# A fused expert, attention and FFN kernel: first FFN product in full rows and 32-row tiles, fp32 rows for q, k and v, v and projection in strips

## The reference

```python
x = x + conv(_gn(x))            # per token: 5 experts of 96x96, the top 2 mixed, leaky relu
t = tokens(x)                   # 16 images x 256 tokens x 96
t = t + attn(_ln_t(t))          # 6 heads of 16, causal
t = t + ffn(_ln_t(t))
...
k = jnp.einsum('btc,hcd->bhtd', x, wk)     # and q, v with wq, wv
out = out.transpose(0, 2, 1, 3).reshape(B, T, C) @ wproj + bproj
...
h = jax.nn.gelu(jnp.einsum('bsd,edh->ebsh', x, w1) + b1[:, None, None, :], approximate=False)
y = jnp.einsum('ebsh,ehd->ebsd', h, w2) + b2[:, None, None, :]
out = jnp.einsum('bse,ebsd->bsd', masked, y)      # masked: softmax gates of the top 2 of 4 experts
```

## Time and profile before

| what | value |
|---|---|
| median of 3 runs | 325.53 us (324.63 to 330.4) |
| profiled execution, its own time | 328.99 us |
| its span | 327.2 us |
| PE busy | 305.1 us, 93% |
| VectorE busy | 242.6 us, 74% |
| ScalarE busy | 217.8 us, 67% |

### The profile page before, as it was taken

The page is one execution under the profiler, slowest core; times in us unless marked ns, Lnnn a source line. Parts: engine busy times, 40 slices in busy tenths (PEclk is TensorE's granted clock), DMA queues, the critical chain, the costliest instruction groups (busy, mean ns, idle before and its releaser), DMA issues.

```text
span 327.2 us, 9038 instructions
## 1 busy us (share of the span) xinstructions
PE 305.1 (93%) x3300; PEld 240.6 (74%) x3300; DVE 242.6 (74%) x1058; ACT 217.8 (67%) x443; POOL 106.9 (33%) x179
## 2 busy tenths in 40 slices
PE   4889888799799999999998999899999999999995
PEld 2655535567679878888876877778887888888884
DVE  5868889888799889998998787368678743653423
ACT  3879676769596895887656844836489398176730
POOL 4563565558600471083070144410442014010000
PEclk9999999989999999999999999989999999999999
DMA  7900072504301120024052006400140010000000
GB/s 181 191 17 1 24 121 62 87 0 107 44 2 40 51 61 2 4 75 99 1 111 63 2 3 125 49 2 1 51 100 3 24 29 2 2 27 2 2 26 24
DMA packets 24199, 14.88 MB, mean 45 GB/s; under 512 B 14399, under 2 KB 24155, under 8 KB 24156
## 3 DMA queue, kind: packets, MB, share of 16 engines
q1 hardware_dynamic: 24156, 14.32, 20.8%
HBM read 3.11 MB, written 1.57 MB: 14 GB/s over the span
## 4 chain that ended last, share of the span: by engine, by line
PE 55%; DVE 9%; SPq 8%; DMA 5%; issue 3%; POOL 2%; ACT 2%; DVEq 0%; POOLq 0%; ACTq 0%
PE PS L974 17%; SPq L497 8%; PE PS L776 7%; PE PS L777 6%; PE PS L778 6%; DMA k_stack<-qk_parts 5%; PE PS L878 3%; PE PS L920 3%; PE PS L902 2%; PE PS L967 2%; PE PS L867 2%; PE PS L829 2%; PE PS L932 1%; PE PS L934 1%; PE PS L906 1%
## 5 line engine op out<-in xcount | busy, mean ns | idle before, releaser
L974 PE MATMUL PS<-w_f,hidden 128*64 128x96 f32 x1536 | 72.1, 251 | 0.0
L769 ACT ACTIVATE hidden<-PS 128x512 f32<-128x512 f32 x96 | 53.5, 599 | 27.2 <-PE PS L778 25.8
L974 PEld LDWEIGHTS PS<-w_f,hidden 128*64 128x64 f32 x1536 | 65.9, 139 | 6.4 <-issue 6.4
L1226 DVE SCALAR_TENSOR_TENSOR res<-PS,weight,res 128x96 f32<-128x96 f32 x128 | 31.4, 309 | 30.4 <-PE PS L974 30.2
L776 PE MATMUL PS<-t_hi,w_hi 97*128 97x512 f32 x96 | 41.7, 435 | 0.0
L1134 DVE CUSTOM_DVE_ANT_0 masked<-PS,causal 128x128 bf16<-128x128 f32 (+1 forms) x120 | 34.9, 352 | 4.3 <-PE PS L878 3.5
L777 PE MATMUL PS<-t_lo,w_hi 96*128 96x512 f32 x96 | 38.1, 397 | 0.0
L778 PE MATMUL PS<-t_hi,w_lo 97*128 97x512 f32 x96 | 38.0, 396 | 0.0
L746 ACT ACTIVATE prob_a<-PS 128x512 f32<-128x512 f32 x48 | 26.0, 600 | 13.4 <-PE PS L902 13.2
L631 POOL TENSOR_SCALAR_AFFINE_SELECT prob_a<-prob_a 128x768 f32<-128x768 f32 x16 | 13.8, 864 | 62.0 <-ACT prob_a L746 62.0
L1095 DVE SCALAR_TENSOR_TENSOR PS<-conv_y,weight,PS 128x96 f32<-128x96 f32 x128 | 30.3, 315 | 1.8 <-ACT PS L698 1.6
(11 more groups left out here) (169 smaller groups left out, 698.7 us busy)
## 6 DMA issues: line engine op xcount, KB each, us to landing
q_stack<-qk_parts SPq DMA_DIRECT2D x48, 96.0 KB, 3.2
k_stack<-qk_parts SPq DMA_DIRECT2D x48, 96.0 KB, 3.7
out_dram<-res SPq DMA_DIRECT2D x8, 192.0 KB, 2.3
X<-in_x_dram SPq DMA_DIRECT2D x4, 192.0 KB, 3.1
X<-in_x_dram SPq DMA_DIRECT2D x2, 384.0 KB, 5.6
hidden<-in_L_ffn_w_dram SPq DMA_DIRECT2D x1, 576.0 KB
w_f<-in_L_ffn_w_dram SPq DMA_DIRECT2D x1, 576.0 KB
hidden<-in_L_conv_We_dram SPq DMA_DIRECT2D x1, 180.0 KB
```

What stands on the lines that cost most here:

```text
L769: act.activation(hidden[:, m, 0:T * P], PS[:, bank("ffn1", n, index), 0:T * P], ACT.Gelu).then_inc(act_emptied["ffn1"], 1)
L974: mm = pe.matmul(PS[strip:strip + STRIP, y, t * C:(t + 1) * C], hidden[:, m, t * P + strip:t * P + strip + STRIP], w2_f[:, m, :], start=Fa ...
L1226: ins = dve.scalar_tensor_tensor(res2[:, t, :], PS[:, y, t * C:(t + 1) * C], weight1[:, t, e:e + 1], res2[:, t, :], ALU.mult, ALU.add).the ...
```

## The change

Five edits, and a new order for all engines:

- `ffn1`: the 3 x 96 rows of the three products are packed. One full matmul of 128 rows holds the 96 high-by-high rows and 32 rows of the low weights, the second the 96 low-by-high rows and another 32, and the last 32 rows of high by low go to a separate matmul with a 32-row operand. The new step `rest1.e` issues these for the three blocks of expert e in a row, from partitions 0, 32 and 64 and into three banks, which stay open until then. b1 becomes the bias of the Gelu.
- The packed rows are laid out by DMA. `t2@n` on SP issues five for each unit once ACT has copied `norm2_t` out, and the first `ffn1` block of the unit waits for all five; `w_w1` issues six for the weights, once.
- `qk` is one fp32 matmul of 512 columns for each of q and k. `v` is fp32 too, in strips of 64 rows; so is `proj`. No low part is made for the first norm, and DVE's `norm1_t` step and GpSimd's `w_qkv` are gone.
- The gate bias is added by DVE in an operation that was there; `turned` and `att_t` now lie in the space of `XT`.
- All lists in `ORDER` are written anew (74 warm products before, 89 after).

```diff
-                    split_product(PS[0:C, bank("qk", n, index), 0:T * P], qk_hi[:, tensor, :], qk_lo[:, tensor, :],
-                                  t1_his[n % 2][:, 0:T * P], t1_los[n % 2][:, 0:T * P]).then_inc(filled["qk"], 1)
+                    pe.matmul(PS[0:C, bank("qk", n, index), 0:T * P], qk_w[:, tensor, :], t1s[n % 2][:, 0:T * P],
+                              start=True, stop=True).then_inc(filled["qk"], 1)
...
                     for t in range(T):
-                        rows = slice(t * P, (t + 1) * P)
-                        mm = split_product(PS[:, bank("v", n), t * C:(t + 1) * C], t1_his[n % 2][:, rows],
-                                           t1_los[n % 2][:, rows], wv_hi[:, :], wv_lo[:, :])
+                        for strip in range(0, P, STRIP):
+                            rows = slice(t * P + strip, t * P + strip + STRIP)
+                            mm = pe.matmul(PS[strip:strip + STRIP, bank("v", n), t * C:(t + 1) * C], t1s[n % 2][:, rows],
+                                           wv_w[:, :], start=True, stop=True, skip_group_check=True)
...
+                            for which, weight in ((2 * image, 0), (1, 1 + image)):
+                                for strip in range(0, P, STRIP):
+                                    rows = slice(half * P + strip, half * P + strip + STRIP)
+                                    mm = pe.matmul(PS[strip:strip + STRIP, bank("proj", n), t * C:(t + 1) * C],
+                                                   att_t[:, which, rows], wproj_r[:, weight, :], start=weight == 0,
+                                                   stop=weight > 0, skip_group_check=True)
...
                     if m == 0:
                         wait_dve(pe, "norm2_t", n)
+                        pe.wait_ge(t2_placed, 16 * T2_COPIES * (n + 1))
                     wait_bank_free(pe, "ffn1", n, index)
                     w = slice(m * P, (m + 1) * P)
-                    split_product(PS[:, bank("ffn1", n, index), 0:T * P], w1_hi[:, w], w1_lo[:, w], t2_his[n % T2][:, 0:T * P],
-                                  t2_los[n % T2][:, 0:T * P]).then_inc(filled["ffn1"], 1)
+                    dst = PS[:, bank("ffn1", n, index), 0:T * P]
+                    pe.matmul(dst, w1_a[:, w], t2_as[n % T2][:, 0:T * P], start=True, stop=False)
+                    pe.matmul(dst, w1_b[:, w], t2_bs[n % T2][:, 0:T * P], start=False, stop=False)
+                elif kind == "rest1":
+                    e = index[0]
+                    for j in range(CHUNKS):
+                        rows = slice(j * REST, (j + 1) * REST)
+                        pe.matmul(PS[:, bank("ffn1", n, (e * CHUNKS + j,)), 0:T * P], w1_c[rows, e, :],
+                                  t2_cs[n % T2][rows, 0:T * P], start=False, stop=True).then_inc(filled["ffn1"], 1)
...
+                elif kind == "t2":
+                    wait_act(sp, "norm2_t", n)
+                    if n >= T2:
+                        wait_filled(sp, "ffn1", n - T2, (BLOCKS - 1,))
+                    t2_a, t2_b, t2_c = t2_as[n % T2], t2_bs[n % T2], t2_cs[n % T2]
+                    sp.dma_start(t2_a[C:P, 0:T * P].bitcast(F32), t2_a[0:REST, 0:T * P].bitcast(F32)).then_inc(t2_placed, 16)
+                    sp.dma_start(t2_b[C:P, 0:T * P].bitcast(F32), t2_a[REST:2 * REST, 0:T * P].bitcast(F32)).then_inc(t2_placed, 16)
+                    for j in range(CHUNKS):
+                        sp.dma_start(t2_c[j * REST:(j + 1) * REST, 0:T * P].bitcast(F32),
+                                     t2_a[2 * REST:3 * REST, 0:T * P].bitcast(F32)).then_inc(t2_placed, 16)
```

More of the change, by code:

```diff
@@ L66 @@
[L66 to L90, removed]
@@ new lines @@
+        prob.1.3@0:6 prob.1.4@0:4 conv.0@5:5 conv.1@5:0 shift@1:1 conv.2@5:6 pv.0@0:4 v@2:2 pv.1@0:3 prob.0.0@1:1
+        prob.0.1@1:5 prob.0.2@1:0 prob.0.3@1:6 prob.0.4@1:4 prob.1.0@1:1 prob.1.1@1:5 proj@0:3 prob.1.2@1:0
+        prob.1.3@1:6 conv.3@5:4 prob.1.4@1:2 warm.3@12:1 score.0.0@2:1 score.0.1@2:5 score.0.2@2:0 score.0.3@2:3
+        score.0.4@2:6 score.1.0@2:2 score.1.1@2:4 norm2_t@0:1 score.1.2@2:5 pv.0@1:0 score.1.3@2:3 norm1_t@3:6
+        score.1.4@2:2 pv.1@1:1 qk.0@3:4 qk.1@3:5 gate2@0:6 ffn1.0@0:0 ffn1.1@0:4 ffn1.2@0:5 rest1.0@0:-1 ffn1.3@0:3
@@ new lines @@
+        ffn1.6@3:1 norm1_t@6:4 score.0.4@5:3 score.1.0@5:2 ffn1.7@3:0 ffn1.8@3:5 rest1.2@3:-1 score.1.1@5:3
+        score.1.2@5:6 score.1.3@5:4 gate2@3:2 prob.0.0@4:3 prob.0.1@4:1 prob.0.2@4:6 score.1.4@5:0 prob.0.3@4:5
+        ffn2.3@2:4 shift@5:0 qk.0@6:3 prob.0.4@4:1 prob.1.0@4:6 prob.1.1@4:5 prob.1.2@4:0 prob.1.3@4:2 qk.1@6:1
+        prob.1.4@4:3 ffn2.0@3:6 pv.0@4:5 pv.1@4:0 prob.0.0@5:2 prob.0.1@5:3 prob.0.2@5:4 prob.0.3@5:6 prob.0.4@5:1
+        v@5:2 v@6:3 prob.1.0@5:5 prob.1.1@5:4 prob.1.2@5:6 prob.1.3@5:2 prob.1.4@5:1 proj@4:0 ffn1.9@3:5 ffn1.10@3:4
@@ new lines @@
+        ffn1.11@3:6 rest1.3@3:-1 score.0.0@6:2 score.0.1@6:1 score.0.2@6:3 pv.0@5:0 pv.1@5:2 score.0.3@6:5 norm2_t@4:1
+        ffn2.1@3:3 score.0.4@6:4 score.1.0@6:0 ffn2.2@3:6 score.1.1@6:2 score.1.2@6:1 score.1.3@6:3 score.1.4@6:5
+        gate2@4:4 norm1_t@7:0 ffn1.0@4:2 ffn1.1@4:1 ffn1.2@4:0 rest1.0@4:-1 ffn1.3@4:3 proj@5:5 shift@6:2 qk.0@7:1
+        qk.1@7:4 ffn2.3@3:2 ffn1.4@4:5 ffn1.5@4:0 rest1.1@4:-1 ffn1.6@4:1 ffn1.7@4:4 ffn1.8@4:6 norm2_t@5:3
+        prob.0.0@6:2 rest1.2@4:-1 ffn2.0@4:5 prob.0.1@6:0 prob.0.2@6:1 prob.0.3@6:4 ffn2.1@4:6 prob.0.4@6:5
@@ new lines @@
+        prob.1.0@6:3 prob.1.1@6:2 prob.1.2@6:0 score.0.0@7:1 score.0.1@7:4 score.0.2@7:5 score.0.3@7:6 gate2@5:3
+        prob.1.3@6:2 prob.1.4@6:1 ffn1.9@4:0 v@7:4 ffn1.10@4:5 ffn1.11@4:2 score.0.4@7:1 rest1.3@4:-1 score.1.0@7:6
+        pv.0@6:4 score.1.1@7:3 score.1.2@7:1 ffn1.0@5:6 score.1.3@7:0 ffn1.1@5:3 score.1.4@7:5 ffn1.2@5:1 rest1.0@5:-1
+        ffn1.3@5:2 ffn1.4@5:0 ffn1.5@5:5 rest1.1@5:-1 pv.1@6:6 shift@7:3 ffn2.2@4:1 ffn2.3@4:2 prob.0.0@7:3
+        prob.0.1@7:0 prob.0.2@7:5 prob.0.3@7:4 prob.0.4@7:1 proj@6:6 prob.1.0@7:2 ffn1.6@5:3 ffn1.7@5:0 ffn1.8@5:5
```

316 lines of the change are left out of this document (168 added, 148 removed).

## The result

The median is **316.02 us** after (315.31 to 319.48, 4 runs) and 327.54 us before (324.63 to 330.4, 4 runs): ratio **0.971**, 95% interval 0.965 to 0.977. The forecast was 317.7 us, with a range of 306 to 330. The profiled execution took 316.23 us, against 328.99.

The account below looks back on a forecast made before the run. PE was taken to bound the kernel from about 110 us on; -6.8 us (PE's stream) - 2.0 (first stretch) + 1.0 (new DMAs and waits) = -7.8, so 325.53 becomes 317.7 us, range 306 to 330.

Parts of the forecast that it names:

- The bound: PE full from about 110 us on, so a shorter matmul stream pays one for one; earlier, the way between engines sets pace.
- First FFN product: `ffn1` with `rest1`: three row tiles run together, full shape-change price paid, 0.53 us; gain 0.18 us times 32 experts, -5.8 us.
- the price of the change: Cost on PE of changing tile shape, into strips and out, read around `ffn2`: 0.29 us, charged to each `rest1`.
- Rival A: Change of shape nearly free for row tiles: `rest1` 0.235 us, `ffn1` gives -15.0 us, total 308.5 us; chance 0.18.
- rival B: The three `rest1` tiles run one after another, shape change paid: 1.00 us, +9.3 instead of -5.8, total 332.8 us; chance 0.08.
- v, proj, q and k: PE steps where PE is full: strips save 1.7 us in `v` and 0.8 in `proj`; fp32 q and k cost 1.5.
- The first stretch: Up to 110 us: dropping DVE's four low-part subtractions for the first norm shortens the way to q, -2.0 us (0 to -3.0).
- The new way: `t2@n`'s five DMAs on SP, their waits, and banks held until `rest1`: +1.0 us, from 0 to +8.
- That just holds: At the last unit, PE's own list, 6.8 us plus `gate2`'s eight matmuls, hides the 7.1 us until the first block.
- rival C: DMAs on SP: stacks or packed rows land 3.2 us late in five issues, PE loses some 8 us, 325 us; chance 0.20.
- The sum: Whole kernel: -6.8 (PE's stream) - 2.0 + 1.0 = -7.8 us, set against the median 325.53, giving 317.7 us.

## Why the prediction was right, and where it was off

**The bound** was read rightly: PE was full from about 110 us on, a shorter stream paid there, and no DMA took its place.

**First FFN product**, -5.8 us forecast, -6.5 in the stream. The mechanism held: together, with the price of the change. Rival A (free change, 0.235) is out by 0.62 us measured, rival B by 0.50 us for three products. The term was mis-sized twice, in opposite directions. I took the change at 0.29 from the strips, and it is 0.62 - 0.235 = 0.38. And I charged it 32 times in full, while at most places the neighbour behind is not a full product of `ffn1`. That the two nearly cancel is luck. With the rule of the Trainium skill (TensorEngine Tiling (Array Packing), Key Properties) that a change of tiling mode drains TensorE, which the prediction weighed, the rows of after agree (0.38 us more than 0.235 for the group and its two changes). The stand-still of the weight load, by which the prediction explained the price, is no sign of it by itself: it also stands still 0.27 us ahead of the bias product, where no price is paid. What the Trainium skill (TensorE: Matmul & The Clock Gate, Measured speedup vs the span model) says of further tiles, a start about 4 ns behind, holds for these row tiles too, at 3 to 4 ns.

**v, proj, q and k**, -1.7, -0.8 and +1.5 forecast; -4.5, -2.5 and +2.2 in the stream. Here are two of the largest misses, both on the safe side. A `v` step took 1.34 us on average before, not the 1.28 of the one that I read, and 0.78 after, not 0.94. One alone between full products:

```profile
237.16 0.40 PE L989 MATMUL PS<-t_b,w_b 128*128 128x512 f32 x1
237.49 0.88 PE L872 MATMUL PS<-wv_w,t 96*64 96x96 f32 x16
238.30 0.51 PE L988 MATMUL PS<-t_a,w_a 128*128 128x512 f32 x1
238.65 0.39 PE L989 MATMUL PS<-t_b,w_b 128*128 128x512 f32 x1
```

It takes 0.81 us and its neighbours 0.10 and 0.11 more than 0.235, about 1.0 in all and near my 0.94; but other units are done in pairs or beside other tiles and share the price of the change, and the neighbours' part stands in other sums. `proj` is 1.46, not 1.59, and was 1.77, not 1.71. I also counted only five and seven of the eight units; the others lie where PE waits and the list holds more warm products (4.1 us more), so there a shorter step need not show in the time. q and k take 2 x 0.43 us a product, as forecast.

**The first stretch**, -2.0 forecast: no gain. Up to 110 us warm products and waiting take 29.8 us before and 30.7 after. The first Gelu of unit 0 starts at 95.7 us, 0.5 later than before, though I had said no later. DVE's four subtractions are gone, but DVE is fuller than before in the two windows shown (18.66 and 18.70 of 20, against 18.08 and 17.01). That taking them off DVE shortens the way to q is the step that failed here: q and k (L862) now wait 1.0 us for ACT's copy, where they waited 0.7 us for the subtraction. What else holds the pace there stays open.

**The new way**, +1.0 forecast: nothing. No wait for the packed rows, and banks held for `rest1` cost nothing. "That just holds" was right: five more DMAs cost 14 us, so rival C was one to two us away at five units, not far off.

**The sum**, -7.8 forecast, is -9.5 against the median it was set on. The lists, which I had counted as nothing, have 0.4 to 3.4 us of it. The two traces differ by more, 12.7 us: the recorded execution of before ran at the lower clock twice (granted 0.91 in the windows from 60 and 200 us), that of after in no window before its end. So `ffn2` became 1.9 us shorter there without any edit: one step at 211 us had run at the lower clock, behind the stack waits, most of which are gone. I had not counted that at all. That the sum came so near is in part luck: v and proj gave more than forecast, the first stretch nothing.

## What to carry to other kernels

Products with few rows are worth packing into row tiles only if they lie in different row groups, and a group of tiles among full products costs 0.38 us beyond its own product here (0.09 going in, 0.20 in the group, 0.10 coming out); put steps with tiles next to each other, and sum the price from the list and not from one place. Where all engines run fixed lists, a step put back on another engine (+21.9 us), or PE's steps moved by one to three places (+17.7 us), can cost far more than itself, above all where the step holds a bank that the list hands on; so test the products and the lists apart, with the waits held equal. A longer wait of PE can cost itself and what the lower clock takes behind it (4.1 us, then 1.6 us more for one `ffn2` step).

## What was unexpected in the hardware

ACT's Gelu of 128 x 512 takes 0.69 us with a bias column and 0.60 without, where I had said that the bias costs nothing because the read of 512 columns sets the time. First after, then before (min/median/max in ns):

```profile
L793 ACT ACTIVATE hidden<-PS,b_t x96: 662/687/713, 95.7 to 306.4; 128x512 f32<-128x512 f32 x96
```

```profile
L769 ACT ACTIVATE hidden<-PS x96: 574/597/645, 95.2 to 316.5; 128x512 f32<-128x512 f32 x96
```

The two kernels with full third products have the same 687 ns, the one with old products in the new lists 597, so it goes with the bias and not with tiles or order. It adds 8 us to ACT (96 times 0.09), and the chain of after that ended last has 1% of ACT in it.

A fp32 product of 96 columns takes 0.107 us a record at full width, but its half-width records run in pairs at about 0.08 us; the narrower form is the faster one, even with its price of change (1.48 us against 1.71 for a `proj`).
